# The output attention gets buffers and a bank of its own, and layer 1's targets are spread from a product's extra column

## What is computed

```
h = relu(layernorm(x)); x = x + L0(h)     # deg * (h Wi + b) + adj (h Wj)
h = relu(layernorm(x)); x = x + L1(h)     # one graph attention, scores from two vectors
h = relu(layernorm(x)); x = x + L2(h)     # 8-head masked attention with q, k, v and an output product
h = relu(layernorm(x)); x = x + L3(h)     # 4 attention heads + elu, joined by W_out, an output attention + elu,
                                          # feed-forward (w1, w2), layer norm with gamma and beta

# a graph attention: Wh = h W ; f1 = Wh a1 (sources) ; f2 = Wh a2 (targets)
# e[i, j] = leaky(f1[i] + f2[j]), masked by adj ; out = softmax(e) Wh
```

## Time and profile before

| what | us |
|---|---|
| median of 3 runs | 1937.42 (1933.59 to 1940.02) |
| the profiled execution, its own time | 1938.1 |
| its span, first to last instruction | 1936.5 |
| PE busy | 1781.1 (92%) |
| PEld busy | 1673.6 (86%) |
| DVE busy | 1646.4 (85%) |
| ACT busy | 1546.9 (80%) |
| POOL busy | 829.5 (43%) |
| DMA, mean share of 16 engines | under 7% |

### The profile page before, as it was taken

One profiled execution on the slowest core, in us unless ns is written; L12 is line 12 of the kernel. 1 busy time (PEld: TensorE's weight loads), 2 busy tenths in 40 slices (PEclk: granted clock), 3 DMA queues, 4 the chain that ended last, 5 costly groups with the idle time before them and its releaser, 6 DMA issues.

```text
span 1936.5 us, 45992 instructions
## 1 busy us (share of the span) xinstructions
PE 1781.1 (92%) x15944; PEld 1673.6 (86%) x15944; DVE 1646.4 (85%) x5519; ACT 1546.9 (80%) x3634; POOL 829.5 (43%) x1332
## 2 busy tenths in 40 slices
PE   0799999999999999999999999999999999999875
PEld 0688889999999899999999999999999999999774
DVE  6577888898998888899898899999888899988863
ACT  2458788888888888888898888889888888888763
POOL 4224444444444444444444444444444444444332
PEclk9889999999999999999999999999999999999996
DMA  5000000000000000000000000000000000000000
GB/s 160 12 23 2 22 23 18 18 23 24 12 24 23 18 18 23 24 13 23 23 18 18 23 24 20 16 23 19 17 23 23 23 12 23 18 18 12 18 18 12
DMA packets 31207, 43.85 MB, mean 23 GB/s; under 512 B 3328, under 2 KB 26880, under 8 KB 30976
## 3 DMA queue, kind: packets, MB, share of 16 engines
q1 hardware_dynamic: 30976, 40.91, 6.4%
HBM read 32.38 MB, written 8.52 MB: 21 GB/s over the span
## 4 chain that ended last, share of the span: by engine, by line
PE 37%; DVE 18%; ACT 13%; issue 9%; DMA 7%; POOL 2%; SPq 1%; DVEq 0%; POOLq 0%; ACTq 0%
PE ps L945 27%; PE ps L974 6%; DMA tbc<-t_dram 6%; DVE tb L1324 3%; DVE pT L1397 3%; ACT ea L844 2%; ACT pb L898 2%; PE ps L1157 2%; ACT tb L830 2%; DVE fu L1361 2%; DMA t_dram<-tb 2%; PE ps L1140 2%; DVE lg L1389 2%; DVE pT L1354 1%; DVE whs L1310 1%
## 5 line engine op out<-in xcount | busy, mean ns | idle before, releaser
L725 POOL TENSOR_SCALAR ea<-ea,rs 128x256 f32<-128x256 f32 x256 | 142.4, 568 | 281.0 <-DVE rs L1345 280.9
L745 POOL TENSOR_TENSOR hid<-fu,hid 128x512 fp32r<-128x512 f32 x128 | 169.5, 1325 | 180.9 <-ACT hid L912 180.9
L898 ACT ACTIVATE pb<-lg,hmin 128x256 f32<-128x256 f32 x512 | 219.8, 501 | 28.6 <-DVE hmin L1389 26.7
L945 PE MATMUL ps<-pT,whs 128*128 128x256 f32 x1536 | 216.5, 291 | 17.0 <-DVE fu L1361 11.2
L945 PE MATMUL ps<-wout,hid 128*128 128x256 f32 x1536 | 226.8, 290 | 1.4 <-ACT hid L912 1.3
L702 POOL TENSOR_TENSOR rstd<-ve,pow_half 128x2 f32<-128x2 f32 x160 | 112.5, 703 | 256.6 <-DVE ve L1241 256.3
L945 PEld LDWEIGHTS ps<-pT,whs 128*128 128x128 f32 x1536 | 192.4, 191 | 32.0 <-issue 16.2
L945 PE MATMUL ps<-wh,hT 128*128 128x256 f32 x1536 | 202.6, 286 | 4.4 <-DVE whs L1310 2.5
L844 ACT ACTIVATE ea<-tb,npeak 128x256 f32<-128x256 f32 x384 | 193.2, 508 | 10.4 <-ACT tb L830 9.3
L945 PEld LDWEIGHTS ps<-wh,hT 128*128 128x128 f32 x1536 | 189.3, 191 | 10.0 <-DVE whs L1310 8.6
L945 PEld LDWEIGHTS ps<-wout,hid 128*128 128x128 f32 x1536 | 195.1, 190 | 2.2 <-ACT hid L912 1.5
(11 more groups left out here) (180 smaller groups left out, 4768.0 us busy)
## 6 DMA issues: line engine op xcount, KB each, us to landing
tbc<-t_dram SPq DMA_DIRECT2D x32, 512.0 KB, 3.8
xin<-x_in SPq DMA_DIRECT2D x32, 256.0 KB, 2.7
out<-xs SPq DMA_DIRECT2D x32, 256.0 KB, 2.2
t_dram<-tb SPq DMA_DIRECT2D x128, 1.0 KB
xs<-a_heads SPq DMA_DIRECT2D x4, 128.0 KB, 6.5
pT<-a_heads SPq DMA_DIRECT2D x4, 128.0 KB, 5.2
lg<-W_out SPq DMA_DIRECT2D x2, 256.0 KB, 5.7
tb<-adj SPq DMA_DIRECT2D x1, 256.0 KB, 2.7
```

The costliest lines, as they stand in the source:

```text
L745: pool.tensor_tensor(hid[g % 2][:, 1], fu[:], f(hid[g % 2][:, 0]), ALU.subtract).then_inc(hid_lo, 1)
L898: last = act.activation(pb[h % 2][:, c, :], lg[h % 2][:, c, :], ACT.Exp, bias=hmin[h % 2][:, c:c + 1], scale=-1.0)
L945: last = pe.matmul(dst, lhs(a, t), rhs(b, t), start=(not low and opens and n == 1), stop=(low is not False and closes and n == terms * len ...
```

## The change

Four things change together.

1. The output attention and the feed-forward get tiles of their own (`who`, `tbo`, `eao`, `pTo`, `st_rows`, and `rb5` for the elu), and they use `BJ` for all: weights, spread, transposes, attended values, output rows. `BX` and `BY` belong to the heads. In exchange the spread waits until the low part of the weights is out of `BJ`, the output's attending product waits for both parts of the probabilities, and `ffn1` is not issued in two parts.
2. Layer 1's own spreading product is gone. The weights' product is issued in a part with the high halves and the rest; DVE copies both extra columns (`cols0`, 128x4), and two fp32 matmuls of `cols0` by `ident` spread the targets, into free columns of the same two banks. The probabilities' minimum, and behind it the high part of the weights, wait for that.
3. The variance's epsilon moves from DVE to POOL, ahead of the power.
4. The scheduler's `GRAIN` and `LEAD` get other values, semaphores are split by kind so that output and heads count apart, and a scratch area for DMA descriptors is made smaller, which makes room for the tiles.

```diff
+        who = sb("who", [P, 2, C, D], F32R)
+        hT5 = who
+        tbo = sb("tbo", [P, C, N])
+        eao = sb("eao", [P, C, N])
+        pTo = sb("pTo", [P, 2, C, N], F32R)
...
-        st_rows = tb3[1][:, 0, :]
+        st_rows = sb("st_rows", [P, N])[:]
...
-        f1p = pT3[HG % PT]
+        f1p = pTo
...
         def probs_bank(g):
-            return BX if g else BX1
+            return BX1 if g == 0 else BX if g < GOUT else BJ
+
+        def attend_bank(g):
+            return BY1 if g == 0 else BY if g < GOUT else BJ
...
-            a("var", n, VE, 0.11, ("aggr", n))
-            a("inv_std", n, PO, 1.1 if n < 4 else 0.78, ("var", n))
+            a("inv_std", n, PO, 1.4 if n < 4 else 1.05, ("aggr", n))
...
-            product(a, "spread", 0, (("rows_hi", 1),), (("rows_lo", 1),))
-            a("wh_first", 0, TE, 0.7, ("rows_lo", 1))
-            a("wh", 0, TE, 0.7, ("tmin", 0), ("wh_first", 0))
-            a("cols", 0, VE, 0.1, ("wh", 0))
+            a("wh_hi_part", 0, TE, 0.47, ("rows_hi", 1), ("x1", 0))
+            a("wh", 0, TE, 0.95, ("wh_hi_part", 0), ("rows_lo", 1))
+            a("cols", 0, VE, 0.12, ("wh", 0))
+            a("spread", 0, TE, 0.22, ("cols", 0))
...
-            transposed(a, TR_HEADS, ("rows", 3), ago("probs_lo", GOUT))
+            transposed(a, TR_HEADS, ("rows", 3), ago("probs_lo", HG))
...
-                a("wh", g, TE, 1.4, ("wh_lo", g - 2) if g > 2 else ("cols", 1) if g == 1 else ago("rows_lo", TR_OUT))
+                a("wh", g, TE, 1.4, ("wh_lo", g - 2) if g > 2 else ("cols", 1) if g == 1 else ago("elu", HG))
...
-            a("cols", g, VE, 1.4, ("join", HG))
-            a("spread", g, TE, 0.45, ("cols", g))
-            weights(a, g, tuple(("exps", C * (g - 2) + c) for c in range(C)))
+            a("cols", g, VE, 1.4, ("join", HG), ago("probs_T", g))
+            weights(a, g, (ago("exps", C * g + C - 1),))
+            a("spread", g, TE, 0.45, ("cols", g), ("wh_lo", g))
             softmax(a, g)
-            attended(a, g, (("tmin", g),), (("elu", HG),))
+            attended(a, g, (("tmin", g),), (("probs_lo", g),))
...
-            product(a, "ffn1", 0, (("rows_hi", TR_OUT),), (("rows_lo", TR_OUT),))
+            a("ffn1", 0, TE, 1.4, ("rows_lo", TR_OUT))
...
-        GRAIN, LEAD = 0.02, (58.0, 49.0, 48.0, 52.0)
+        GRAIN, LEAD = 0.2, (34.0, 34.0, 33.0, 33.0)
...
         def rows_bank(t):
-            return (BX1, BX1, BA, BB, BX, BY)[t]
+            return (BX1, BX1, BA, BB, BX, BJ)[t]
...
-                def spread_targets(g, u, low):
...
-                    last = product(bank(BY1)[:, 0, :], lambda a, t: w1g[:, a, t, D + 1:WC].broadcast_to([P, P]),
-                                   lambda b, t: hT1[:, b, t, :], C, RIGHT_FRESH, low)
...
+                def spread_first_targets(g, u):
+                    pe.wait_ge(cols_ready(g), u + 1)
+                    for c in range(C):
+                        last = pe.matmul(wh1_banks()[:, c, WC:WC + P], cols0[:, c, 1:2].broadcast_to([P, P]),
+                                         ident[:], start=True, stop=True)
+                    last.then_inc(dbc_done(g), 1)
...
-                        dve.tensor_copy(cols0[:], wh1_banks()[:, :, D]).then_inc(cols_ready(0), 1)
+                        dve.tensor_copy(cols0[:], wh1_banks()[:, :, D:WC]).then_inc(cols_ready(0), 1)
...
-    nc = bacc.Bacc("TRN2", target_bir_lowering=False, num_devices=1)
+    nc = bacc.Bacc("TRN2", target_bir_lowering=False, num_devices=1, dynamic_dma_scratch_size=1024)
```

More of the change, by code:

```diff
@@ L144, in wh_parts @@
         def wh_parts(g):
-            return wp1 if g == 0 else whs[(g - 1) % HG]
+            return wp1 if g == 0 else whs[g - 1] if g < GOUT else who
         def as_heads(t):
@@ L169, in source_cols @@
         def source_cols(g):
-            return cols0[:] if g == 0 else cols3[:, :, g - 1] if g < GOUT else colso[:, 0, :]
+            return cols0[:, :, 0] if g == 0 else cols3[:, :, g - 1] if g < GOUT else colso[:, 0, :]
         stored = [sem(f"stored{k}") for k in range(XB)]
@@ L582, in section @@
             name = name.removesuffix("_hi_part")
-            if name in ("stats", "aggr", "var", "inv_std", "rows"):
+            if name in ("stats", "aggr", "inv_std", "rows"):
                 return OF_NORM[k]
@@ L622, in head @@
         def head(g, u):
-            return u + 1 if g == 0 else of(u, g - 1, GOUT)
+            return of(u, g - 1, HG) if 1 <= g <= HG else u + 1
         def head_chunk(g, c, u):
@@ L631, in each, with gat @@
             return [sem(f"{name}{k}") for k in range(n)]
-        def gat(name):
-            pair = each(name, 2)
-            return lambda g: pair[min(g, 1)]
+        FIRST, HEADS, LAST = "first", "heads", "last"
+        def gat(name, *kinds):
+            of_kind = {kind: sem(f"{name}_{kind}") for kind in kinds or (FIRST, HEADS, LAST)}
+            return lambda g: of_kind[FIRST if g == 0 else HEADS if g <= HG else LAST]
         rows_ready, rows_T, rows_hi, rows_lo = (each(n, 6) for n in ("rows_ready", "rows_T", "rows_hi", "rows_lo"))
-        var_ready, rstd_made, rstd_ready = each("var_ready", 5), each("rstd_made", 4), each("rstd_ready", 5)
+        mv_ready, rstd_made, rstd_ready = each("mv_ready", 5), sem("rstd_made"), each("rstd_ready", 5)
         deg_ready, bo_ready, beta_ready = sem("deg_ready"), sem("bo_ready"), sem("beta_ready")
@@ L1027, in spread_output_targets, with first_weights, chunk @@
                     last.then_inc(dbc_done(g), 1)
[L1029 to L1037 removed]
+                def first_weights(_, u, low):
+                    def chunk(c, low):
+                        return product(wh1_banks()[:, c, 0:WC], lambda a, t: hT1[:, a, t, blk(c)],
+                                       lambda b, t: w1g[:, b, t, :], C, LEFT_FRESH, low)
+                    if not low:
+                        pe.wait_ge(rows_hi[1], u + 1)
+                        chunk(1, low)
+                    else:
+                        pe.wait_ge(rows_lo[1], u + 1)
+                        chunk(1, low)
+                        chunk(0, None).then_inc(wh_done(0), 1)
```

167 lines of the change are left out of this document (80 added, 87 removed).

## The result

The changed kernel takes 1877.32 us (median of 4 runs, 1876.46 to 1879.78) against 1936.43 for the kernel before on the same chip: ratio 0.9696 (0.9677 to 0.9715), 3.0% faster. I had forecast 1907 with a range from 1878.

The account below looks back on a forecast made before the run. It took PE, 97.3% busy, as nearly the bound, though over half the ending chain ran elsewhere. 1750.2 + 8 + 11.6 - 20 = 1749.8, plus 156 of drain and 1.6 outside the span: 1907 us, range 1878 to 1945.

Parts of the forecast that it names:

- Part 3: Output attention apart: opens the loop between batches, -0.8 us a period (bounds 0 and -1.5), output chain 3 us longer.
- part 4: Drain behind batch 29's colso: 156 us against 186.3, with work ahead of that colso growing by 8 us.
- the two waits: Next batch's score rows and heads waiting for the output's probabilities and rows; removing them opens the loop.
- the bare loop: Output attention to next batch's heads to its output attention: 49.3 us bare in a period of 55.9.
- Part 1: Layer 1's spread on PE: 0.87 us removed, 0.37 added, net -0.50 a batch, -16 us (bounds 0 and -28).
- Part 2: More products cut in two on PE: 5 cuts at 0.08 us, +0.4 us a batch.
- The two waits of the earlier trace that were to stay: PE's waits inside the heads' `BX` (probabilities' low part, 11.6 us) and `BY` (elu, 7.9 us), claimed to stay.
- The longer output chain: Spread +1.5, attending product +0.8, `ffn1` +0.7: +3 us a batch, hidden in the middle, exposed at the end.
- Part 5: The rest: POOL's extra instruction a norm and smaller descriptor scratch, both taken as nothing.
- A: Rival: full queues set the steady period, only the drain gains, 1927 us (1925 to 1943); chance 0.24.
- B: Rival: PE waits at the new spread and output's transposes, up to 1.3 us a period, 1960 us; chance 0.18.
- C: Rival: PE's whole 3.4 us unfilled is open, 2.2 a period get filled, 1872 us; chance 0.08.

Follow-up runs that it names:

- edges_back: Changed kernel with two waits put back (next batch's transposed rows and second head's weights wait for the output attention), constants set anew: 1928.5 us, ratio 0.9945.
- spread_tuned: Kernel before with layer 1's new spread alone, GRAIN and LEAD set for it: 1936.0 us, ratio 0.9980.
- before_tuned: Kernel before with only GRAIN and LEAD set anew by search: 1936.9 us, ratio 0.9985.
- old_spread_tuned: Changed kernel with layer 1's old spread, GRAIN and LEAD set for that: 1877.8 us, ratio 0.9680.
- before_six_more: Kernel before with 6 matmuls a batch of layer 1's weights' product issued twice: ratio 0.9994.
- buffers_alone: Kernel before with only the output attention's own tiles and bank; old spread, epsilon on DVE, old GRAIN and LEAD: 1952.3 us, ratio 1.0079.
- after_old_spread: Changed kernel with layer 1's old spread, at the changed kernel's GRAIN and LEAD: 1929.1 us, ratio 0.9954.
- after_old_lead: Changed kernel with the old GRAIN and LEAD: 1983.6 us, ratio 1.0230.
- buffers_tuned: Kernel before with the output attention's own tiles and bank alone (old spread, epsilon on DVE), GRAIN and LEAD set for it: 1880.7 us, ratio 0.9686.
- old_var_tuned: Changed kernel with the epsilon back on DVE, GRAIN and LEAD set for it: 1864.0 us, ratio 0.9612.

## Where the prediction was right, and where it was wrong

**The step that failed** is the size that I gave the opened loop. Part 3 takes -0.8 us a period, bounded by the visible idle, and part 4 counts the work ahead of batch 29's colso, the fill in it, by PE's work alone (+8). Measured, the period fell by 1.51 us, and batch 4's colso came 3 us later where my terms put it 22 later. That is 15 and 19 us, less 4 that the drain gave back: the 30 us between 1907 and the time. The direction, the drain and the two waits as the main cause were right. The 0.8 by itself is what the two waits cost in the middle (0.81, edges_back); what I had put at nothing is all else that own tiles and a bank give there, another 0.7 us a period, and which part does that, or whether the constants do, stays open.

**What bounds the kernel: half right.** I saw that the chain ran more through other queues than through PE and that the bare loop was 49.3 us, and then still summed PE's work as the time. The runs say that before, PE's work had nearly no price (0 for 6 matmuls more, 7 of 32 for 8 fewer). I also took the 49.3 us as a loop with 7 us of air. edges_back shows that closing it costs 0.81 us a period all the same. I read it so that in a period where four other batches compete for PE, the loop's steps queue behind theirs, and 49 bare is 56 in company; that is argued.

**Part 1, the spread: wrong, 0 for -0.50 a batch** (-16 us), on the lower bound that I had named. In the kernel before PE was not the bound, so nothing was to be had (spread_tuned: 0.9980, before_tuned: 0.9985). In the changed one less was to be had than I took. From its start to the next start the new spread takes 0.70 us in the mean of 22 periods, not 0.37. The group by itself (whole program), and the wait of the weight loads behind it (290 to 1700 us, 26 periods):

```profile
L1034 PE MATMUL ps<-ident,cols 128*128 128x128 f32 x128 | 22.3, 298 | 0.3 <-DVE cols L1304 0.3
...
PEld ps L1160 <- DVE pT L1416: 5.1, 18, 0.3
```

PE doesn't wait for the copy of the columns. It waits, in 18 of 26 periods, behind the spread: layer 2's scores, next in its queue, are held by DVE's low part of the probabilities, 0.2 us a period. That leaves 0.5 for the spread, as the colso now has (mean 0.50, before 0.36). So 0.37 us a batch were saved without that wait, and 0.17 with it; 0.37 is 12 us as PE's work and some 9 at what PE's work is worth in the changed kernel. old_spread_tuned, 3 us faster by its ratio with a period longer by 0.16, can't tell that from nothing, since constants alone move the time by as much.

**Part 2, the cuts: no fixed price of +0.08 each.** From start to start, `wo` takes 1.43 us in two groups now and 1.42 in one in edges_back (1.60 in one before); `wp,pT` takes 1.50 in two and 1.51 in one. But in the kernel before, `whs,wf` takes 1.62 where it is cut and 1.53 in the seven periods where it is whole, while `whs,pT` takes 1.51 both ways. So a cut costs 0 to 0.1 us, by what stands beside it. Groups per period rose from 61.3 to 66.5 by the trace (which leaves out buffer numbers), and the part of the period outside visible waits fell from 54.74 to 53.74: whatever the cuts cost was outweighed. The errors of parts 1 and 2 (16 and up to 11.6 us) nearly cancel, which is luck.

**Part 3, the opened loop: the right mechanism, mis-sized.** The measured period fell by 1.51. Of it 0.59 is visible idle (1.28 to 0.69 a period over 22 periods), 0.2 to 0.4 is work that the spread no longer is (old_spread_tuned gets its gain without that), and the rest came out of what I had counted as changes from group to group. I read that rest as short waits behind semaphores that a freer order fills, and no fixed price; that it can be filled is shown by before_six_more, that it is made of such waits is argued. The two waits of the earlier trace rows that were to stay went as well: edges_back doesn't bring them back at their old places either (0.2 and 0.4 us), so they belonged to the old order. The longer output chain is right: from the end of the last batch's join to the end of the program 32.8 us pass where 29.5 did, +3.3 against my +3. Its three terms are there as waits of PE: 3.01 us ahead of the last colso where there were 1.56, 1.50 ahead of the attending product where there were 0.69, and 1.41 ahead of `ffn1` where there were 0.69, so +1.5, +0.8 and +0.7 as forecast. The `ffn1` of before, then two rows of now:

```profile
1922.38 2.93 PE L945 MATMUL ps<-whs,wf 128*128 128x256 f32 x12 [0.69 <-ACT whs L794]
...
1853.81 2.90 PE L966 MATMUL ps<-who,pTo 128*128 128x256 f32 x12 [1.50 <-DVE pTo L1373]
...
1861.31 2.93 PE L966 MATMUL ps<-who,wf 128*128 128x256 f32 x12 [1.41 <-DVE who L1263]
```

**Part 4, the drain: right.** 47, 44, 34 and 31.3 us were forecast, 49.6, 45.6, 35.0 and 29.8 measured, 160 for 156. That this drain belongs to the two waits is shown by edges_back, which has the old steps with tiles, bank and work new. Wrong was the work ahead of it. By my terms (a pipeline deeper by some 22 us, and -0.5 + 0.4 - 0.8 us a period) batch 4's colso should have come 22 us later, and it comes 3 later. The first colso is 14 us later (189.3 against 175.1), but the next three periods of the fill take 54.7, 54.1 and 54.5 us, where they took 57.9, 60.3 and 56.0: the same loop was closed in the fill, and I had priced only its work. edges_back bears that out: with the two waits back its first colso is at 176.6, and the next three periods take 56.8, 60.5 and 57.9. (Batch 4's colso is then at 351.8, as the closed loop lets less work in at the start and gets through it more slowly.) That is 19 us of the miss. The other 15 are the middle, where the period fell by 1.51 and not by 0.9 (25 periods). The drain took back 4.

**Part 5: the constants were not priced.** I named the scheduler's numbers in the change and gave them no term. As a gain that was right (before_tuned: 0.9985). But for a kernel whose edges are edited they are the largest term of all: by the ratios 76 us in buffers_alone, 53 in old_spread_tuned against after_old_spread, 103 from the changed kernel to after_old_lead. The epsilon at nothing was within what can be told.

**The rivals.** A is refuted: the middle gained 38 us. B's places are there in the queue and cost nothing in the middle: the output's transposes stand 7.1 us behind the colso (896.28 to 903.36) without a wait, and the copy is there when PE comes to the spread (0.3 us in the whole program). The steps of the period in between were longer than I had counted, 3.5 us to the spread and not 2.7. C named the size of the time nearly right (1872), and the right kind of reserve, the time that is unfilled and not seen as idle. But in the middle its sign was a distance of 53.6 us, the forecast's 55.0, and 54.53 was measured, nearer to the forecast; that C's time came out is in part luck, since the fill and not the middle gave the rest. By the Trainium skill (Perfetto Trace Analysis, Identifying the Most-Contended Engine) the weight loads' busy time tells headroom and the matmuls' does not. The windows agree: PE's busy time grew 1.1% and its weight loads' 2.5%, and the matmuls in the stretch 2.6%. The middle gained 38 us, and only some 15 of them are matmul idle that went away (38 to 23 us in the 1400). I gave this 0.08, since I asked how much idle was visible and not how elastic the time was. What C does not say is by which part the reserve is opened; for a good half that is the loop, which I had in my forecast. That DVE paces the middle, my last reservation, is refuted by buffers_tuned, which keeps all of DVE's work.

**What stays open.** Tiles and bank were only tried together. Of the 61 us, some 10 in the sum and 18 in the middle are not the two waits', and whether another buffer gives them or the constants do is not told. Nor is it told whether old_var_tuned's lead comes from the epsilon or from its constants.

## What to carry to other kernels

A busy share does not tell what an engine's work is worth; a few instructions more and a few less on it do, and two such runs of the kernel before would have shown that a PE at 97% did not set its pace. Look then for waits that reach from the end of one batch to the start of the next: here two of them cost 20 us in the middle and 32 in the drain, and the trace named other places. Where constants set the order of the queues, no part of a change can be judged by undoing it alone; give each variant constants of its own, and the old kernel too.

## What the runs showed that I had not expected

- A matmul's busy time does not give its slot: in the middle the colso's records have a mean of 288 ns now (274 before), but 0.50 us pass to the next start where 0.36 did. What sets this is not known; another kind of work follows it in the two queues.
- Cutting a product's 12 matmuls into two groups has no fixed price on PE: 0.01 us for `wo`, 0.09 for `whs,wf`.
- The same work in another order of the queues took 1877 to 1984 us in the changed kernel, and 1881 to 1952 with tiles and bank alone.
- DVE's minima of the heads (256 instructions of 128x256) have a mean of 428 ns where it was 515. edges_back, at 1928 us, has 429, so this is no part of the gain. What sets it was not tested. Before and after, the whole program:

```profile
L1324 DVE CUSTOM_DVE_ANT_0 tb<-tbc,mask3p 128x256 f32<-128x256 f32 x256 | 122.5, 515 | 43.0 <-DMA tbc<-t_dram 42.7 <-issue 0.4
...
L1343 DVE CUSTOM_DVE_ANT_0 tb<-tbc,mask3p 128x256 f32<-128x256 f32 x256 | 100.0, 428 | 4.3 <-DMA tbc<-t_dram 4.3
```
